# Two local-attention layers of 16 tiles each, joined into one run of 32 tiles with the feed-forward work inside its steps

## The reference, cut to what matters

```
for l in range(2):
    h = shift_token(x)               # features 64..127 come from the token before
    q, k, v = split(h @ wqkv[l])     # 8 heads of 64
    q, k = l2norm(q)*qs, l2norm(k)*ks
    q, k = rotary_xpos(q, k)
    o = local_attention(q, k, v)     # windows of 64: a window sees itself and the one before
    x = x + o @ wo[l]
    h = layernorm(shift_token(x)) @ w1[l] + b1[l]
    a, g = split(h)                  # 341 each
    x = x + (a * gelu(g)) @ w2[l] + b2[l]
```

## Time and profile before

| what | value |
|---|---|
| median of three runs | 725.07 us |
| profiled execution, time | 724.48 us |
| its span | 722.7 us |
| PE busy | 579.6 us (80%) |
| DVE busy | 503.7 us (70%) |
| POOL busy | 424.4 us (59%) |
| ACT busy | 349.8 us (48%) |
| mean granted TensorE clock | 0.896 |

### The profile page before, as it was taken

One profiled execution on the slowest core, in us unless ns is written; L12 is line 12 of the kernel. 1 busy time (PEld: TensorE's weight loads), 2 busy tenths in 40 slices (PEclk: granted clock), 3 DMA queues, 4 the chain that ended last, 5 costly groups with the idle time before them and its releaser, 6 DMA issues. The chain is left out here.

```text
span 722.7 us, 13195 instructions
## 1 busy us (share of the span) xinstructions
PE 579.6 (80%) x4922; PEld 410.7 (57%) x4922; DVE 503.7 (70%) x1103; ACT 349.8 (48%) x607; POOL 424.4 (59%) x342
## 2 busy tenths in 40 slices
PE   4579999679288999998699799999986964787712
PEld 3247777547135777767557366777774642555511
DVE  2877888555867888884643788888755445867776
ACT  2334555363255665665453565666645423444333
POOL 5654674271379999991310999999903115656620
PEclk9659999979688999999999999999999985878965
DMA  8600000000011111110000111111100000000001
GB/s 264 179 1 1 1 1 1 1 1 1 0 34 26 39 38 32 31 31 10 1 1 0 45 31 32 31 30 39 32 2 0 1 1 0 0 1 1 1 0 58
DMA packets 16141, 18.15 MB, mean 25 GB/s; under 512 B 4261, under 2 KB 10831, under 8 KB 16079
## 3 DMA queue, kind: packets, MB, share of 16 engines
q1 hardware_dynamic: 14639, 14.70, 7.9%
q10 hardware_dynamic: 1440, 2.61, 1.1%
HBM read 8.01 MB, written 1.05 MB: 13 GB/s over the span
## 5 line engine op out<-in xcount | busy, mean ns | idle before, releaser
L222 POOL TENSOR_TENSOR rstd<-rstd,minus_half 128x4 f32<-128x4 f32 x32 | 33.8, 1058 | 159.9 <-DVE rstd L216 159.8
L1295 POOL TENSOR_TENSOR qk<-qk 128x512 f32<-128x512 f32 x64 | 80.3, 1275 | 33.8 <-DVE qk L1181 33.8
L1299 POOL TENSOR_TENSOR rn<-n,minus_half 128x16 f32<-128x16 f32 x32 | 93.8, 2932 | 2.7
L1178 DVE TENSOR_TENSOR qk<-ps,rt 128x512 f32<-128x512 f32 x64 | 44.0, 687 | 45.1 <-ACT sq L1099 31.2
L1137 ACT ACTIVATE ptb<-ps 128x512 f32<-128x512 f32 x64 | 34.8, 595 | 72.5 <-PE ps L902 72.5
L1304 POOL TENSOR_TENSOR qk<-qk,rn 128x512 f32<-128x512 f32 x64 | 65.5, 1044 | 2.5
L610 POOL TENSOR_TENSOR xy<-xy,rd 128x616 f32<-128x616 f32 x32 | 38.9, 1217 | 42.7 <-DVE rd L479 42.7
L1099 ACT ACTIVATE sq<-ps 128x512 f32<-128x512 f32 x64 | 37.7, 598 | 20.8 <-PE ps L868 7.6
L563 PE MATMUL ps<-pt,vbd_a 128*128 128x128 f32 x320 | 41.7, 288 | 6.8 <-ACT pt L577 6.8
L563 PEld LDWEIGHTS ps<-pt,vbd_a 128*128 128x128 f32 x320 | 39.0, 200 | 13.8 <-issue 12.9
L872 PEld LDWEIGHTS ps<-consts,qk 128*128 128x128 f32 x256 | 29.4, 141 | 27.0 <-issue 16.1
(11 more groups left out here) (196 smaller groups left out, 1620.8 us busy)
## 6 DMA issues: line engine op xcount, KB each, us to landing
vv<-vv SPq DMA_DIRECT2D x62, 130.0 KB, 2.3
wqkv<-in_wqkv SPq DMA_DIRECT2D x1, 1536.0 KB, 16.2
x<-in_x SPq DMA_DIRECT2D x4, 256.0 KB, 7.6
out<-xy SPq DMA_DIRECT2D x4, 256.0 KB, 2.3
w_b<-in_w_b SPq DMA_DIRECT2D x1, 682.0 KB
tmat<-in_tmat SPq DMA_DIRECT2D x1, 616.0 KB, 7.7
w<-in_w ACTq DMA_DIRECT2D x1, 512.0 KB, 3.8
rot<-in_c_rot ACTq DMA_DIRECT2D x1, 512.0 KB, 8.5
```

The costliest lines, as they stand in the source:

```text
L1178: dve.tensor_tensor(qk[:, n % 3, kind].rearrange("p (h d) -> p h d", d=DH), src.rearrange("p (h d) -> p h d", d=DH), rt[:, layer, j, i:i + ...
L1295: pool.tensor_tensor(w, w, qk2[:, kind], ALU.add).then_inc(done, 1)
L1299: pool.tensor_tensor(rn[:, k, :], n2[:, k, :], minus_half[:], ALU.pow).then_inc(rn_done, 1)
```

## The change

Both layers become one loop of 32 tiles (NT2 = 32) with 8 groups (U2 = 8), whose steps run from 0 to 42. Weights are chosen by n // 16. The feed-forward work of group g is placed into the steps: moves and statistics in step 9 + 4g, `norm` and `flip` in 10 + 4g, the three chunks in 11, 12 and 13 + 4g, `project` in 14 + 4g, and `finish` in 15 + 4g. For groups 4 to 7 `turn(g)` comes in step 15 + 4(g-4), so right behind the `finish` that it needs; for the first layer's groups 1 to 3 it comes in steps 3, 7 and 11.

- `project` stands at the end of PE's step, ahead of the next tile's Q. In the step behind it k is turned after the wo projection, since it uses the same bank.
- On DVE `finish` and the output sum stand between the K products and the Q products. Before, both products came first.
- A chunk's two matmuls use the banks of q and k of the step (4 and 5); V of the step waits until DVE has read them. There is one `gel` and one `hidt` buffer instead of two; each chunk waits for the one before.
- The shifted features come by three DMAs per group from y into `hs` (in the space of wa1), and no longer by matmuls. ACT normalises the whole 128 features of the four tiles, DVE does none.
- Gelu on ACT stands behind Exp in three of four steps.
- POOL does `pool_rstd` at the start of a flip step and the bias sum (`biased`) at its end.
- Of stage A's closing work on DVE, `norm_y(1)`, `add_ffn(3)`, `add_x(2)` move to the end of step 0, `norm_y(2)`, `add_x(3)` to step 1, `norm_y(3)` to step 2; `add_x(0)` now comes before `add_ffn(1)`. ACT's halves of `norm_y` are at the ends of its steps.

The diff, cut to its core:

```diff
-                        add_ffn(0)
-                        add_ffn(1)
-                        add_x(0)
...
+                        add_ffn(dve, 0)
+                        add_x(dve, 0)
+                        add_ffn(dve, 1)
+                        norm_y(dve, 0)
+                        add_x(dve, 1)
+                        add_ffn(dve, 2)
...
-                hidt = qk[:].rearrange("p a k d -> p (a k d)").rearrange("p (k c s) -> p k c s", k=2, c=NH)
-                gel = pb[:].rearrange("p k h q -> p (k h q)")[:, 0:2 * S].rearrange("p (k s) -> p k s", k=2)
-                for layer in range(DEPTH):
+                hidt = qt[:].rearrange("p u s -> p (u s)")[:, 0:NH * S].rearrange("p (c s) -> p c s", c=NH)
+                gel = qt[:, U - 1, :]
+                hs = wa1[:].rearrange("p (j d) -> p j d", d=D)
+                FLIP, HIDDEN, PROJECT = 10, 11, 14
...
+                    def due(n, at):
+                        g, r = divmod(n - at, TPB)
+                        return g if r == 0 and 0 <= g < U2 else None
+                    def chunk(n):
+                        g, c = divmod(n - HIDDEN, TPB)
+                        return (g, c) if c < NH and 0 <= g < U2 else None
...
 PE, step n
-                            for n in range(NT + LR):
+                        for n in range(PROJECT + TPB * (U2 - 1) + 1):
+                            behind = due(n - 1, PROJECT) is not None
...
+                            if behind and LS <= n < NT2 + LS:
+                                pe.wait_ge(y_done, done_by(n - 1, PROJECT))
+                                shape_k(n)
...
+                            if chunk(n) is not None:
...
+                                hidden(*chunk(n))
+                            turned_now = n < NT2 - 1 and n % TPB == TPB - 1
+                            if turned_now:
+                                pe.wait_ge(q_prod, n + 1)
+                                turn((n + 1) // TPB, bank_q)
...
+                            if due(n, FLIP) is not None:
...
+                                flip(due(n, FLIP))
...
+                            if due(n, PROJECT) is not None:
+                                pe.wait_ge(ont_done, min(n - LO + 1, NT2))
+                                pe.wait_ge(kt_done, min(n - LS + 1, NT2))
+                                project(due(n, PROJECT))
...
 SP
+                        def move(g):
+                            t0 = TPB * (g % U)
+                            sp.wait_ge(r_done, TPB * (g + 1))
...
+                            sp.dma_start(hs[1:P, :, 64:128], y[0:P - 1, t0:t0 + TPB, 64:128]).then_inc(hs_in, 16)
+                            sp.dma_start(hs[0:1, 1:TPB, 64:128], y[P - 1:P, t0:t0 + TPB - 1, 64:128]).then_inc(hs_in, 16)
+                            sp.dma_start(hs[:, :, 0:64], y[:, t0:t0 + TPB, 0:64]).then_inc(hs_in, 16)
...
 ACT, step n
+                            if due(n, FLIP) is not None:
+                                norm(due(n, FLIP))
+                            if chunk(n) is not None:
+                                gelu(*chunk(n))
+                            if n < NT2 - 1 and n % TPB == TPB - 1:
+                                turned((n + 1) // TPB, bank_q)
...
 DVE, step n
+                                products(n, bank_k, 1).then_inc(k_prod, 1)
+                            if due(n - 1, PROJECT) is not None:
+                                finish(due(n - 1, PROJECT))
+                            if LR <= n < NT2 + LR:
...
+                                dve.tensor_tensor(y[:, m % NT, :], bank_r, y[:, m % NT, :], ALU.add).then_inc(r_done, 1)
...
+                                products(n, bank_q, 0).then_inc(q_prod, 1)
...
+                            if chunk(n) is not None:
+                                hidden(*chunk(n))
...
+                            if due(n, FLIP - 1) is not None:
+                                stats(due(n, FLIP - 1))
+                            if n == 0:
+                                norm_y(dve, 1)
+                                add_ffn(dve, 3)
+                                add_x(dve, 2)
```

More of the change, by code:

```diff
@@ L634, in flamingo_kernel, with add_ffn, add_x, norm_y @@
                 hidt = sb("hidt", [P, 2, NC, S], scope=scope)
[L636 to L639, removed]
+                with stage("a_chain", "x_chain", "ap_chain", "var1", "rstd1", "var2", "rstd2", "var3", "rstd3", "nmr1", "nmr3", "xn_dve", "axn_act",
+                           "axnt_raw", "axnt_done", "h_raw", "h_done", "a_proj", "f_used", "a_base", "yn_dve", "yn_act") as (block, sems):
+                    (a_chain, x_chain, ap_chain, var1, rstd1, var2, rstd2, var3, rstd3, nmr1, nmr3, xn_dve, axn_act,
+                     axnt_raw, axnt_done, h_raw, h_done, a_proj, f_used, a_base, yn_dve, yn_act) = sems
+                    xv = []
+                    def add_ffn(dve, u):
+                        dve.wait_ge(a_proj, u + 1)
+                        dve.wait_ge(a_base, u + 1)
+                        ins = dve.tensor_tensor(base[:, sl(u), :], bank[6 + u % 2].rearrange("p (j d) -> p j d", d=D),
+                                                base[:, sl(u), :], ALU.add)
+                        ins.then_inc(f_used, 1)
+                        dve.wait_ge(f_used, u + 1)
+                        dve_stats(dve, xv[0], u, base, var2)
+                    def add_x(dve, u):
+                        for n in range(TPB * u, TPB * (u + 1)):
+                            xv[0].do(dve.scalar_tensor_tensor(out=base[:, n, :], in0=base[:, n, :], scalar=mv[:, n, 0:1],
+                                                          in1=gated_rows[:, 0, :], op0=ALU.subtract, op1=ALU.mult))
+                        xv[0].sync()
+                        dve.wait_ge(rstd2, u + 1)
+                        for n in range(TPB * u, TPB * (u + 1)):
+                            xv[0].do(dve.scalar_tensor_tensor(out=x[:, n, :], in0=base[:, n, :], scalar=rstd[:, n:n + 1],
+                                                          in1=x[:, n, :], op0=ALU.mult, op1=ALU.add))
+                        xv[0].sync()
+                        dve_stats(dve, xv[0], u, x, var3)
+                    def norm_y(dve, u):
+                        dve.wait_ge(rstd3, u + 1)
+                        dve_nmr(dve, u, nmr3)
+                        for n in (TPB * u, TPB * u + 1):
+                            dve_norm(dve, n, y[:, n, :], x[:, n, :]).then_inc(yn_dve, 1)
+                    def norm_y_rest(act, u):
+                        act.wait_ge(nmr3, u + 1)
+                        for n in (TPB * u + 2, TPB * u + 3):
+                            act_norm(act, n, y[:, n, :], x[:, n, :]).then_inc(yn_act, 1)
@@ L651, in norm @@
                                     ins.then_inc(done, 1)
[L653 to L672, removed]
                         dve_stats(dve, v, 0, base, var1)
@@ L776, in gelu @@
                                 if u >= 2:
[L777 removed]
+                                    act.wait_ge(a_proj, u - 1)
                                 act.activation(hidt[:, u % 2, c, :], bank[2 + c], ACT.Gelu, bias=b1_a[:, c:c + 1]).then_inc(h_done, 1)
[L780 to L781 removed]
+                        norm(0, xn, base, nmr1, axn_act)
+                        norm(1, xn, base, nmr1, axn_act)
                         flipped(0)
                         flipped(1)
[L784 removed]
+                        norm(2, xn, base, nmr1, axn_act)
                         gelu(0)
[L786 removed]
+                        norm(3, xn, base, nmr1, axn_act)
                         flipped(2)
@@ L791, in _ @@
                         gelu(3)
[L792 to L795, removed]
+                        norm_y_rest(act, 0)
             with ExitStack() as scope:
```

953 lines of the change are left out of this document (468 added, 485 removed).

## The result

The changed kernel takes 742.36 us (median of 4 runs, 737.49 to 743.75) against 725.14 (724.55 to 727.01) beside it: ratio 1.0222 [1.0177, 1.0267], slower by 2.2%. The forecast was 709 with 692 to 728, and it was wrong in its sign. The profiled execution took 743.75 us with a span of 742.0, 19.3 more than before in both. First the head of its page: the span, and the busy time of each engine.

What follows compares the result with a forecast made beforehand. PE was taken as the bound at 8.25 us a step, POOL just behind. Tile 31's K products at 497.65 plus a 76.6 tail gave 574.2 against 589.73: 15.5 us off 724.48, so 709, range 692 to 728.

Steps and rivals of the forecast that it cites:

- the term for SP's moves: Three moves per group on SP: 2.3 us for one, 3.5 for three; DVE asks 6 us later, so no cost.
- The bound of 7 us: Upper bound for a group's moves, one after another; the lower bound was 2.3 us, one transfer.
- One sign of being wrong: The forecast is wrong if a group of four takes over 48 or under 42, or the tail over 85.
- Tail: From tile 31's K products to the layers' end: 72.6 us, some 4 more for half clock, 76.6 against 76.45 before.
- Head: Tile 0's K products at 185.8 instead of 201.37; closing work in steps 0 to 2 leaves a lead of 8.3.
- Steps: Full steps in groups of four: 8.65, 15.0, twice 10.35 and 0.1, 44.45 us; tile 31 at 497.65, lead 15.6.
- The price of 0.4 for DVE's chain: In a chunk step V waits for DVE's gate product: 10.35 us against PE alone at 9.97, cost 0.4.
- Rival A: PE keeps its own pace, 10.45 instead of 11.1 a step over 22 steps, no half clock: 691 us; chance 0.17.
- rival C: Small waits of 0.7 us a step over 22 steps eat the win: 724.5; chance 0.18 together with Rival D.
- Rival B: ACT's table loads pass DVE's chain: 1.3 us more in 24 steps, 31 us, 740; chance 0.15 with the skill's rule.
- The drain of its second form: By the skill's rule two drains more make Gelu end 2.76 later: 36 us in 18 steps, 745; chance 0.03.
- Rival D: Layer 1's first tile waits for group 0's closing sum, halting once per group: 721; chance 0.18 together with rival C.

Runs made afterwards that it cites:

- e1: Changed kernel with each group's 127-row move cut into two moves of 112 and 15 rows; 714.99 us, ratio 0.9858.
- e6: Changed kernel with its 127-row move cut into four moves of 127 rows, one per tile; 735.87 us, ratio 1.0148.
- e10: e1 with the two pieces cut into 113 and 14 rows instead of 112 and 15; 738.74 us, ratio 1.0181.
- e5: e1 with all of DVE's closing work, and POOL's powers with it, ahead of step 0; 714.86 us, ratio 0.9850.
- e4: e1 with DVE's output sum behind Q's products again, as in the kernel before; 711.40 us, ratio 0.9812.
- e2: Changed kernel with Gelu computed as Exp, so no other table in a chunk step (values differ); 741.06 us, ratio 1.0216.
- e3: e1 with Gelu computed as Exp (values differ); 712.08 us, ratio 0.9809.
- e7: e4 with group 6's projection put ahead of the last flip; 712.44 us, ratio 0.9792.
- e8: e7 with the last group's chunks starting on a free bank without waiting for the product before; 708.66 us, ratio 0.9745.
- e9: e8 with five matmuls into a bank nobody reads, ahead of the last flip; 705.52 us, ratio 0.9732.

## Why the prediction was wrong

**The step that failed** is the term for SP's moves: "2.3 us for one transfer, 3.5 taken for three; DVE asks for them 6 us later". By it the moves were hidden in the steps and cost nothing there. DVE did ask 6.3 us after the sum; the 3.5 was wrong. The row was that of another shape. It is a copy of 64 whole rows (V's halves, 130 KB); the new one has 127. The three took 10.7 us from L1103's issue (360.02 in the group shown) to the statistics that asked for them (370.68), DVE stood 36.8 us in 8 groups, and the bound of 7 us that I gave ("one after another") was broken too, since it took each of the three at no worse than the row.

The Trainium skill (DMA: Bandwidth & Descriptors, section Why a DMA increments its semaphore by 16 and not by 1) gives the rule in its paragraph on how many engines a DMA uses: the largest number up to 16 that divides the outer size on both sides, with 127 partitions as its example for one engine. The trace agrees (share 0.07), and so do e1, e6 and e10. It spoke straight against this change, and I had not weighed it. One sign of being wrong that the forecast named did come: the tail took 90.0 us, over 85.

Where its price lies, from K's products of tile 0 to the end of the layers (changed kernel against e1, whose code differs in nothing else): 419.9 against 393.5, 26.4 us. Tiles 0 to 9 0.8, 9 to 15 7.7 (first wait, at step 9, 4.3), 15 to 31 10.6, from there to the last output sum 2.1 (3.7 without a dip of the clock in e1 that stands under *Tail*), the tail behind it 5.2. The two ratios, 1.0222 and 0.9858, are 3.6% or 26.4 us apart: one cause accounts for all of the loss of 19 us and more. Of the 33.2 us of waiting that e1 takes away, some 5 to 7 had come back in the flip steps and in slack.

The other steps, read in e1, where the failed one is out of the way:

- *Head.* K products of tile 0 at 185.5 (forecast 185.8), of tile 3 at 211.9 (211.0), of tile 9 at 261.9 (260.1). The positions were right. But e5 shows that the late closing work bought little: with tile 0 9.6 later, tile 3 is 1.6 later and tile 31 2.0. The layers' end is the same chiefly because e1's profiled execution had the dip of the clock that stands under *Tail*; the medians, 714.99 and 714.86, show no gain from it either. The lead of tile 0 was real and almost worthless: steps 0 to 2 took 26.4 us with the closing work inside and 18.4 without.
- *Steps.* Groups of four 44.0 (forecast 44.45): 10.5, 10.5, 8.46, 14.57 against 10.35, 10.35, 8.65, 15.0. Tile 31 at 496.3 (497.65). The price of 0.4 for DVE's chain in a chunk step is e4's 0.36. **Rival A** (PE alone, 10.45 a step, 41.8 a group) is out, and **rival C** too: the walk left out no 0.7 a step.
- *Tables.* 38 loads, nearly hidden: e2 no gain, e3 about 3 us. **Rival B** had come out near the measured time, at 740, and for that reason looked like the winner until e2; it is refuted. The drain of its second form does not show (1.30 from load to function, and the load of 350.95 starts as the Exp before it ends).
- *One run.* The closing sum of 382.18 lies in its step, and e1's steps have no halt. **Rival D** is out.
- *Tail.* Forecast 76.6, e1 82.7 (496.3 to 579.0), with the failed step 90.0. Output sums of the drain steps took 53.2 instead of 49.0, the row of single pieces behind them 29.4 instead of 27.6. Of the first 4.2 us, 1.6 are group 5's projection, first in e1, then in e5, which has the same code there:

```profile
534.05 4.52 PE L951 MATMUL ps<-w_b,qt 128*128 128x128 f32 x24 [0.95 <-ACT ont L1198]
```
```profile
536.07 2.94 PE L960 MATMUL ps<-w_b,qt 128*128 128x128 f32 x24 [0.95 <-ACT ont L1207]
```

  The granted clock was 0.66 in e1 from 533 to 536, and 1.00 in e5 from 535 to 541; e5, e7, e8 and e9 take 51.6 for the drain steps. Of the other 1.8 us, 1.35 are the moves once more: from tile 31's output sum to the statistics they took 4.85 us even when spread, and the sum had 3.5. All this is the second, smaller error: 6 us, which leaves e1 at 579.0 against 574.2, and at 715 against 709. So even without the failed step the time would have come out 6 us over the forecast, within its own range of 700 to 717.

Kernels with the same code ahead of tile 0 have its K products at 185.5 to 190.7 (e1, e7), with a granted clock of 0.94 and 0.88 from 50 to 100 us and of 0.92 and 0.84 from 150 to 182. So a difference of 5 us between single executions says nothing here, and the comparisons above go by stretches or by medians.

Not settled: which wait sets the 2.6 us of the drain steps that are left, why the moves landed 1.8 us later in e9, and with it whether its filler matmuls shorten the whole. Nor was it tried to issue the unshifted half ahead of the shift.

## What to carry to other kernels

Before a DMA takes the place of a matmul, look at the size of its outer dimension on both sides, not at its bytes: a shift by one partition has 127 rows, and it ran on one engine, 8 us for 127 KB; cut into 112 and 15 rows it left 3.6 us of waiting out of 36.8. Price a new transfer only from a row of the same shape. When a rival's time agrees with the measured one, test it all the same: the tables stood within 3 us of the result, and taking them out of the changed kernel gained nothing that can be told from noise. And when two executions end alike, compare them stretch by stretch: e9's gain of 1.6 us was hidden by a wait ahead of it.

## What the runs showed of the hardware

- Such a move also holds up the queue that issued it: behind the 127 rows the next issue on SP took 6.45 us instead of 0.7 (5.7 behind 113 rows, 0.95 behind 112), in all 8 groups. In e6, with four moves of a quarter each, the issues took 1.29 at the median.
- 127 KB over one DMA engine went at 16 GB/s; the 128 KB of the unshifted half went at 129 in the one microsecond from 583.1, in the last group.
- PE at half clock after 5.27 us of idleness took twice as long for a pair of matmuls with as many columns, 2.04 against 1.02. Five matmuls that nobody reads, put into the gap, made the stretch from the flip to the last projection 9.77 us instead of 11.38 in the profiled executions; the whole kernel showed no gain.
